# Each head's queries written at their place by half-height instructions, with two query transfers a pair in place of three

## The reference: one macaron layer

```python
x = x + 0.5 * ffn(layernorm(x), W_fc, W_proj)
x = x + attention(layernorm(x), w_qkv, w_out, b_out)
x = x + 0.5 * ffn(layernorm(x), W_fc, W_proj)

# attention: 16 heads of 64
q, k, v = heads(x @ w_qkv)
sim  = (q * 64**-0.5) @ k.T - |i - j| * slope[head]     # causal
out  = softmax(sim) @ v  ->  @ w_out + b_out
# ffn: y = relu(x @ W_fc.T)**2 @ W_proj.T, then five steps of a spiking neuron:
mem = 0.9 * mem + y - (mem > 1);  spike = (mem_new > 1);  result = mean of the five spikes
```

## Time and profile before

| | before |
|---|---|
| median of three runs | 1670.28 us |
| profiled execution, its own time | 1667.52 us |
| span of the profile | 1665.7 us |
| TensorE, matmul busy | 1584.9 us, 95% |
| weight loads busy | 1293.9 us, 78% |
| VectorE busy | 1181.6 us, 71% |
| ScalarE busy | 1284.4 us, 77% |
| GpSimd busy | 955.3 us, 57% |
| DMA queue q1 | 162.12 MB, 44.9% of 16 engines |
| query transfers | 384 of 256 KB, 2.9 us from issue to landing |

### The profile page before, as it was taken

One profiled execution on the slowest core, in us unless ns is written; L12 is line 12 of the kernel. 1 busy time (PEld: TensorE's weight loads), 2 busy tenths in 40 slices (PEclk: granted clock), 3 DMA queues, 4 the chain that ended last, 5 costly groups with the idle time before them and its releaser, 6 DMA issues.

```text
span 1665.7 us, 34863 instructions
## 1 busy us (share of the span) xinstructions
PE 1584.9 (95%) x10902; PEld 1293.9 (78%) x10902; DVE 1181.6 (71%) x4272; ACT 1284.4 (77%) x3446; POOL 955.3 (57%) x1258
## 2 busy tenths in 40 slices
PE   5799999999999999999999999999999999999995
PEld 3677878878787887878878787887878788787774
DVE  6475695867858587785858869586785858778563
ACT  2588787888878788787878878788887878878781
POOL 3455565665656566565656656566565656656551
PEclk7899999999999999999999999999999999999998
DMA  2455444445444445454445544444544444545430
GB/s 77 92 115 115 93 106 92 102 99 115 102 97 101 100 97 116 89 118 92 87 110 107 115 96 102 95 103 100 113 101 96 101 104 96 112 91 110 105 75 12
DMA packets 80518, 164.35 MB, mean 99 GB/s; under 512 B 12880, under 2 KB 30928, under 8 KB 80208
## 3 DMA queue, kind: packets, MB, share of 16 engines
q1 hardware_dynamic: 80336, 162.12, 44.9%
HBM read 6.88 MB, written 4.19 MB: 7 GB/s over the span
## 4 chain that ended last, share of the span: by engine, by line
PE 78%; DVE 11%; DMA 4%; issue 4%; POOL 1%; ACT 1%; SPq 1%; DVEq 0%
PE bank L404 13%; PE bank L389 13%; PE bank L375 8%; PE bank L376 8%; PE bank L359 7%; PE bank L447 7%; PE bank L455 6%; PE bank L360 6%; PE bank L361 6%; DMA queries<-queries 4%; DVE drive L637 2%; DVE negsc L577 2%; DVE spikes L634 2%; DVE queries L691 1%; DVE negmem L640 1%
## 5 line engine op out<-in xcount | busy, mean ns | idle before, releaser
L933 POOL TENSOR_TENSOR prob<-prob,rsum 128x512 f32<-128x512 f32 (+3 forms) x1024 | 761.6, 760 | 641.4 <-DVE rsum L586 640.4
L818 ACT ACTIVATE prob<-negsc,negmax 128x512 f32<-128x512 f32 (+3 forms) x1024 | 575.8, 565 | 114.0 <-DVE negmax L577 107.7
L577 DVE CUSTOM_DVE_ANT_0 negsc<-bank,alibi 128x512 f32<-128x512 f32 (+3 forms) x1024 | 466.4, 474 | 6.4 <-PE bank L376 6.4
L829 ACT COPY probT<-bank 128x512 f32<-128x512 f32 x640 | 362.9, 588 | 63.0 <-PE bank L389 62.8
L375 PE MATMUL bank<-keys,queries 128*128 128x256 f32 (+2 forms) x1024 | 346.7, 350 | 34.5 <-issue 25.5
L586 DVE RECIPROCAL rsum<-sums 128x1 f32<-128x1 f32 (+1 forms) x768 | 121.4, 158 | 353.5 <-PE bank L376 336.1
L389 PE MATMUL bank<-ident,prob 128*128 128x128 f32 x2560 | 364.0, 273 | 1.3 <-POOL prob L933 1.3
L389 PEld LDWEIGHTS bank<-ident,prob 128*128 128x128 f32 x2560 | 300.6, 140 | 25.9 <-POOL prob L933 4.6
L376 PE MATMUL bank<-keys,queries 128*128 128x256 f32 (+2 forms) x1024 | 318.3, 325 | 0.0
L404 PE MATMUL bank<-probT,vals 128*64 128x512 f32 (+3 forms) x2048 | 303.9, 439 | 0.7 <-ACT probT L829 0.7
L404 PEld LDWEIGHTS bank<-probT,vals 128*64 128x64 f32 x2048 | 135.5, 136 | 159.7 <-issue 135.6
(11 more groups left out here) (82 smaller groups left out, 2198.1 us busy)
## 6 DMA issues: line engine op xcount, KB each, us to landing
queries<-queries SPq DMA_DIRECT2D x384, 256.0 KB, 2.9
keys<-k_lo SPq DMA_DIRECT2D x256, 128.0 KB, 2.7
keys<-keys SPq DMA_DIRECT2D x128, 128.0 KB, 2.3
x_in<-in_L_attn_x_dram SPq DMA_DIRECT2D x16, 256.0 KB, 3.2
out_dram<-x SPq DMA_DIRECT2D x16, 256.0 KB, 2.4
prob<-in_L_attn_w_qkv_dram SPq DMA_DIRECT2D x1, 1536.0 KB, 8.3
wo<-in_L_attn_w_out_dram SPq DMA_DIRECT2D x1, 512.0 KB, 10.4
probT<-in_L_ffn_W_fc_dram SPq DMA_DIRECT2D x1, 256.0 KB, 3.4
```

What stands on the lines that cost most here:

```text
L577: ins = dve.tensor_tensor_reduce(negsc[:, k % 3, col:col + WIDTH[i]], src, alibi[:, 2 * p + h, N - WIDTH[i]:N], 1.0, MASKED, ALU.add, ALU.min,
L818: ins = act.activation(prob[:, p % 2, h, PCOL[i]:PCOL[i] + WIDTH[i]], negsc[:, k % 3, col:col + WIDTH[i]], ACT.Exp, bias=negmax[:, p % 2, ...
L829: act.copy(probT[:, turn_slot(p, t), :], turn_bank[(len(TRUNS) * p + t) % 2][:, :]).then_inc(s_turned_out, 1)
L933: ins = pool.tensor_tensor(pr, pr, rsum[:, p % 2, seg:seg + 1].to_broadcast([P, WIDTH[i]]), ALU.mult)
```

## The change

ScalarE rounds the queries by two instructions of 64 rows: first head 1's (rows 64 to 127, into head 1's place), then head 0's (rows 0 to 63, into head 0's place). VectorE subtracts in the same way, each half waiting for its own `s_qhi[h]` and raising its own `s_qlo[h]`. Each head then lies in one half of its rows at its own place, and SyncE copies it to the other half: one transfer of 256 KB a head, each after its `s_qlo[h]`, with nothing between them (`both_queries`). The old third transfer and its wait on `s_twice[.][1]` are gone. The side bank is free when `s_qlo[0]`, the later of the two, is raised. In a slot with queries first SyncE issues both query transfers, the two of head 1's keys, and then head 0's keys; with keys first the two key transfers, both query transfers, and head 0's keys.

```diff
--- before.py
+++ after.py
@@ -157,8 +157,9 @@
 
         s_scores, s_biased, s_exp, s_rsum, s_norm = (sem(n) for n in ("s_scores", "s_biased", "s_exp", "s_rsum", "s_norm"))
         s_turned, s_turned_out, s_pv, s_att = (sem(n) for n in ("s_turned", "s_turned_out", "s_pv", "s_att"))
-        s_q, s_qhi, s_qlo, s_k, s_khi, s_klo, s_v, s_vals = (
-            sem(n) for n in ("s_q", "s_qhi", "s_qlo", "s_k", "s_khi", "s_klo", "s_v", "s_vals"))
+        s_qhi, s_qlo = ([sem(f"{n}{h}") for h in range(2)] for n in ("s_qhi", "s_qlo"))
+        s_q, s_k, s_khi, s_klo, s_v, s_vals = (
+            sem(n) for n in ("s_q", "s_k", "s_khi", "s_klo", "s_v", "s_vals"))
 
         s_fc, s_relu, s_hid, s_y, s_ysb, s_spk = (
             {w: sem(f"{n}{w}") for w in (1, 3)} for n in ("s_fc", "s_relu", "s_hid", "s_y", "s_ysb", "s_spk"))
@@ -185,7 +186,7 @@
 
         def twice_no(b, p, h):
 
-            return (b * (PAIRS // 2) + (p // 2 + 1)) * (16, 32)[h]
+            return (b * (PAIRS // 2) + (p // 2 + 1)) * 16
 
         def keys_no(b, p, h):
 
@@ -217,7 +218,7 @@
 
             if kind in "qk":
                 p = (s + 1) % PAIRS
-                return (s_qlo if kind == "q" else s_klo), pair_no(b, p)
+                return (s_qlo[0] if kind == "q" else s_klo), pair_no(b, p)
             if kind == "v":
                 return s_vals, v_no(b, s // 2, i)
             if kind in ("t1", "t2", "t3"):
@@ -292,11 +293,11 @@
 
                 top, low = slice(0, DH), slice(DH, P)
                 par = p % 2
-                def low_queries():
-                    sp.wait_ge(s_qlo, pair_no(b, p))
-                    for rows in (top, low):
-                        sp.dma_start(queries[rows, par, 1, :, :].bitcast(F32),
-                                     queries[low, par, 0, :, :].bitcast(F32)).then_inc(s_twice[par][1], 16)
+                def both_queries():
+                    for h, (there, here) in ((1, (top, low)), (0, (low, top))):
+                        sp.wait_ge(s_qlo[h], pair_no(b, p))
+                        sp.dma_start(queries[there, par, h, :, :].bitcast(F32),
+                                     queries[here, par, h, :, :].bitcast(F32)).then_inc(s_twice[par][h], 16)
 
                 def low_keys():
                     sp.wait_ge(s_khi, pair_no(b, p))
@@ -304,25 +305,18 @@
                     sp.wait_ge(s_klo, pair_no(b, p))
                     sp.dma_start(keys[low, par, 1, :].bitcast(F32), k_lo[low, :].bitcast(F32)).then_inc(s_keys[par][1], 16)
 
-                def top_queries():
-                    sp.wait_ge(s_twice[par][1], twice_no(b, p, 1))
-                    sp.dma_start(queries[low, par, 0, :, :].bitcast(F32),
-                                 queries[top, par, 0, :, :].bitcast(F32)).then_inc(s_twice[par][0], 16)
-
                 def top_keys():
                     sp.wait_ge(s_keys[par][1], keys_no(b, p, 1))
                     sp.dma_start(keys[low, par, 0, :].bitcast(F32), k_lo[top, :].bitcast(F32)).then_inc(s_keys[par][0], 16)
 
                 if q_first(p):
-                    low_queries()
+                    both_queries()
                     low_keys()
-                    top_queries()
                     top_keys()
                 else:
                     low_keys()
-                    low_queries()
+                    both_queries()
                     top_keys()
-                    top_queries()
 
             def slots(b, par, last):
 
@@ -687,8 +681,10 @@
                 src = side_bank[n % 2][:, :]
                 if kind == "q":
                     p = (s + 1) % PAIRS
-                    dve.wait_ge(s_qhi, pair_no(b, p))
-                    dve.tensor_tensor(q_lo[:, p % 2, 0, :], src, q_hi[:, p % 2, 0, :].bitcast(F32), ALU.subtract).then_inc(s_qlo, 1)
+                    for h, rows in ((1, slice(DH, P)), (0, slice(0, DH))):
+                        dve.wait_ge(s_qhi[h], pair_no(b, p))
+                        dve.tensor_tensor(q_lo[rows, p % 2, h, :], side_bank[n % 2][rows, :], q_hi[rows, p % 2, h, :].bitcast(F32),
+                                          ALU.subtract).then_inc(s_qlo[h], 1)
                 elif kind == "k":
                     p = (s + 1) % PAIRS
                     dve.wait_ge(s_khi, pair_no(b, p))
@@ -841,9 +837,12 @@
                 if kind in "qk":
 
                     p = (s + 1) % PAIRS
-                    dst, made, done = (q_hi, s_q, s_qhi) if kind == "q" else (keys, s_k, s_khi)
-                    act.wait_ge(made, pair_no(b, p))
-                    act.copy(dst[:, p % 2, 0, :], src).then_inc(done, 1)
+                    act.wait_ge(s_q if kind == "q" else s_k, pair_no(b, p))
+                    if kind == "k":
+                        act.copy(keys[:, p % 2, 0, :], src).then_inc(s_khi, 1)
+                    else:
+                        for h, rows in ((1, slice(DH, P)), (0, slice(0, DH))):
+                            act.copy(q_hi[rows, p % 2, h, :], side_bank[n % 2][rows, :]).then_inc(s_qhi[h], 1)
                 elif kind == "v":
                     q = s // 2
                     act.wait_ge(s_v, v_no(b, q, i))
```

## The result

| | before | after |
|---|---|---|
| median | 1669.97 us (4 runs, 1668.06 to 1671.84) | 1723.88 us (4 runs, 1721.56 to 1724.77) |
| ratio, 95% interval | | 1.0321 (1.0303 to 1.0339), 3.2% slower |
| profiled execution, its span | 1667.52, 1665.7 us | 1723.86, 1722.1 us |

A forecast was written before the change was run, and what follows sets the result against it. TensorE sets the time, with one wait at slot 0 and VectorE full from slot 6 to slot 0. 2.4 us a batch over 14 batches, 33.6, less 2 for the first, gives +31.6: 1702 us, range 1666 to 1722.

The forecast's parts named there:

- the price of an added instruction: One more instruction a pair on each engine: 0.46 us on ScalarE, 0.60 on VectorE, behind another one.
- third rival: Each change of rows also loses VectorE's overlap, 0.08 us twice a pair: 0.4 a batch, 1707 us; chance 0.16.
- The path: TensorE's lateness followed slot by slot through one batch, slots 1 and 2 undelayed: 2.4 us a batch.
- slots 6 and 7: VectorE, full from slot 6, goes from 0.6 to 1.2 us late; slot 0 then starts 1.2 late.
- Halves at full price: Half-height instructions keep 512 columns and cost what full height does, means near 580 and 690 ns.
- Slots 4 and 5 together 0.6 late: ScalarE full in slot 4, a stall of about 0.5 at slot 5's transposes; TensorE 0.6 us late after slot 5.
- the forecast's 1.2 by way of `vals`: Slot 0: ScalarE's `vals` comes 1.2 us late, and the value product waits for it without cover, 1.2 more.
- The wait of slot 0 "about where it is": TensorE's wait at slot 0's first score, ended by head 1's keys: some 1.8 - 1.1 + 1.2 us.
- The third transfer and its wait worth nothing in steady batches: Removing them wins nothing at the batch boundary: 768 KB still end with head 1's keys.
- no steady batch waits for queries: In steady batches no score waits for queries; only while the pipeline fills does one.
- The first batch 2 us faster: Pipeline filling, slot 2: without the third transfer and its wait, about 2 us gained, once.

The follow-up runs named there:

- experiment 11: Experiment 9 with only ScalarE's added cast over the low 64 rows, VectorE's added subtraction over all 128: 1712.41 us, 1.0263.
- experiment 12: Experiment 9 with only VectorE's added subtraction over the low 64 rows, ScalarE's added cast over all 128: 1727.52 us, 1.0354.
- experiment 9: Experiment 5 plus six small identity products that TensorE does in its wait at the start of slot 0: 1702.63 us, 1.0200.
- experiment 7: The kernel after for the three pairs made in slots 1, 2 and 3, the kernel before for the five others: 1673.26 us, 1.0032.
- experiment 2: The kernel before, full-height cast and subtraction kept, with the two unchained query transfers of the kernel after: 1668.21 us, 0.9997.
- experiment 10: Experiment 9 with both the added cast and the added subtraction over the low 64 rows alone: 1731.11 us, 1.0371.
- experiment 5: The kernel before plus one full-height cast a pair on ScalarE and one full-height subtraction on VectorE, three transfers kept: 1716.23 us, 1.0286.
- experiment 6: The kernel before with only VectorE's subtraction cut into two halves, low rows first; ScalarE's cast and the three transfers kept: 1725.97 us, 1.0347.

## Why the prediction went wrong

**The step that failed** is the price of an added instruction. "I take 0.46 and 0.60" was read from neighbours that all start at row 0. Measured it is 0.71 and 0.82, since both halves begin at other rows than the instruction in front. The text had this mechanism as its third rival, under "Against it: no row", and made it too small in three ways: 0.16 us a pair where 0.22 were lost (a gap of 0.03 comes with the lost overlap), on VectorE alone where ScalarE loses 0.25 too (9.8 us by itself, experiment 11), and in slots 6, 7 and 0 alone where slot 4 takes 0.69 of VectorE's 1.60 a batch (experiment 12). 1707 instead of 1702 was all that it gave.

**The path was right in its slots and its sum, less so in its parts.** With the price that the forecast had, experiment 9 gives 2.38 us a batch for 2.4, and experiment 7 that slots 1 to 3 don't grow. But two errors cancel in that sum: slots 6 and 7 add 0.91 us where 0.6 were forecast, slot 0 adds 0.78 where 1.2 were. Point by point:
- Halves at full price, 580 and 690 ns: right, 580 and 689. The argument for it was weaker than the outcome: rows of 256 and 512 columns at one height differ in elements as well, so they could not tell columns from elements.
- Slots 4 and 5 together 0.6 late: 0.59 at the forecast's price, 1.31 after. That VectorE's lost overlaps count in slot 4 was not seen: the text put slot 4 down to ScalarE, whose own lost overlaps count in slot 6 above all (experiment 11).
- Slot 0: the forecast's 1.2 by way of `vals` is 0.78 at its price and 1.50 after. The timeline of TensorE has the wait for `vals`, but a larger one ahead of it, for VectorE's `xn`, which the text lacked:

```profile
348.76 0.47 PE L369 MATMUL bank<-keys,queries 128*128 128x512 f32 x1 [1.55 <-issue]
...
358.10 0.63 PE L425 MATMUL bank<-ident,xn 128*128 128x128 f32 x4 [0.69 <-DVE xn L604]
360.35 0.39 PE L353 MATMUL bank<-wv_hi,xa_hi 128*128 128x256 f32 x1 [0.27 <-ACT vals L851]
```

- The wait of slot 0 "about where it is": nearly, 1.56 us a batch for 1.73, where the forecast's sum was 1.9.
- The third transfer and its wait worth nothing in steady batches: right (experiment 2). That no steady batch waits for queries has one exception in the trace before, batch 6, whose wait of 1.89 us a query transfer ended. Beside the halves the two transfers are worth 8 us: 1732 with three, 1724 with two. The profiled executions differ by 12.6 us in span (1734.7 and 1722.1), of which 6.9 lie in the 14 batches (1444.2 and 1437.4 us in their windows), 3.3 ahead of them and 2.4 behind; a batch at full clock and with the usual slot 7 is 102.65 us long in the one and 102.67 in the other. So most of the 6.9 us is in the batches that fall to the lower clock, 4 for 1, and in three whose slot 7 takes 13.3 us for 12.4. Why these are longer wasn't tried.
- The first batch 2 us faster: wrong. It is 0.7 us longer (93.75 for 93.02). The term itself was of the right size, for with the transfers alone (experiment 2) the first batch takes 90.90 us; that the added work would take more than that there was left out.
- The last batch and the tail were left out of the sum. They are 4.0 us longer: 2.0 in the last batch's slots 0 to 6, 2.0 from its slot 7 to the end.

The miss in the profiled span, 56.4 for 31.6 us, is then 14 times 1.31 (3.71 less 2.4 a batch), which is 18.3, with 2.5 at the start and 4.0 at the end. The first part is in the main the price of the lost overlaps (experiments 9 to 12); the two others are terms that the sum had wrong or lacked.

## What to carry to other kernels

Price an added instruction by the step from its neighbour's start to the next one's start, and ask whether it starts at the same row: halves of a tile over the same 512 columns cost here what the whole did (689 and 580 ns), and on VectorE and ScalarE each change of the start row from 0 to 64 or back cost a further 0.11 and 0.13 us. Before splitting an instruction to save a transfer, look whether that transfer ends a wait; here hardly a batch behind the first waited for it, and experiment 2 gained nothing in the median. When two versions of a kernel are compared, look at TensorE's granted clock stretch by stretch before the difference is put down to the edit: in experiment 5 it fell behind slot 0's wait in 11 of 14 batches, at about a microsecond each.

## What the hardware showed that was not expected

- ScalarE loses its overlap at a change of the start row as VectorE does: a gap of 0.025 us in place of an overlap of 0.10. In experiments 9 and 10 the step from the cast of the queries to the copy behind the added cast is 0.99 and 1.24 us:

```profile
340.97 0.58 ACT L855 CAST queries<-bank 128x512 fp32r<-128x512 f32 x1
341.44 0.63 ACT L857 CAST more_hi<-wq_hi 128x512 fp32r<-128x512 f32 x1
341.96 0.60 ACT L838 COPY probT<-bank 128x512 f32<-128x512 f32 x1
```

```profile
343.02 0.58 ACT L855 CAST queries<-bank 128x512 fp32r<-128x512 f32 x1
343.62 0.62 ACT L857 CAST more_hi<-wq_hi 64x512 fp32r<-64x512 f32 x1
344.26 0.59 ACT L838 COPY probT<-bank 128x512 f32<-128x512 f32 x1
```

- The clock behind an idle TensorE. It fell behind the wait of slot 0 in some batches and not in others, and the length of the wait doesn't tell which. In batch 4 of the kernel before it stayed at 2.4 GHz (1.00) behind 1.89 us; in batch 3 of experiment 6 it was at 1.2 GHz nearly throughout (0.51) behind 1.75 us (for each the timeline, then the window of the three microseconds behind the wait):

```profile
441.08 0.47 PE L375 MATMUL bank<-keys,queries 128*128 128x512 f32 x1 [1.89 <-issue]
...
441.05:444.05 3.00, 2.97 (x16) 2.56 (x17) 2.90 (x12) 2.04 (x9) 1.75 (x4) 1.00 0.79 188
```

```profile
350.38 0.74 PE L377 MATMUL bank<-keys,queries 128*128 128x512 f32 x1 [1.75 <-issue]
...
350.35:353.35 3.00, 2.97 (x10) 2.61 (x11) 2.90 (x7) 2.04 (x7) 1.50 (x3) 0.51 0.58 125
```

In the kernel after it fell once, behind 1.57 us; in experiment 7 it stayed at 1.00 once behind 3.03 us. What decides was not found. With the small products in that wait (1.50 us of them in experiment 9) it stayed at 1.00 in all 14 batches of each of experiments 9 to 12.
